# TensorE's program as loops of two heads, with paired buffers, quartered bias windows and 64-wide near products

## The reference

```python
attn = jnp.einsum('bhid,bhjd->bhij', q, k)
qL = jnp.einsum('bhid,hdm->bhim', q, rpe_k_table)
attn = attn + jnp.take_along_axis(qL, idx, axis=-1)
kL = jnp.einsum('bhjd,hdm->bhjm', k * scale, rpe_q_table)
attn = attn + jnp.swapaxes(jnp.take_along_axis(kL, idx, axis=-1), 2, 3)
attn = jax.nn.softmax(attn, axis=-1)
out = jnp.einsum('bhij,bhjd->bhid', attn, v)
S = jax.vmap(lambda a, seg: jax.ops.segment_sum(a, seg, num_segments=NUM_BUCKETS))(a_t, rp)
out = out + jnp.einsum('inbh,hnd->bhid', S, rpe_v_table)
```

## Time and profile before

| | us |
|---|---|
| runs | 1524.4, 1528.8 (median), 1531.9 |
| span of the profiled execution | 1522.0 |
| attention heads 0 to 29 | about 180 to 776 |
| experts | about 780 to 845 |
| heads 30 to 63 and projection | about 845 to 1522 |

### The profile page before, as it was taken

The page is one execution under the profiler, slowest core; times in us unless marked ns, Lnnn a source line. Parts: engine busy times, 40 slices in busy tenths (PEclk is TensorE's granted clock), DMA queues, the critical chain, the costliest instruction groups (busy, mean ns, idle before and its releaser), DMA issues. The chain is left out here.

```text
span 1522.0 us, 75140 instructions
## 1 busy us (share of the span) xinstructions
PE 1325.6 (87%) x32698; PEld 895.9 (59%) x32698; DVE 1111.2 (73%) x2461; ACT 797.9 (52%) x1408; POOL 541.3 (36%) x552
## 2 busy tenths in 40 slices
PE   2785399999999999988989899999999999999887
PEld 1352256666666666655668565666666666666555
DVE  7684378888888888887764676777777767777762
ACT  1332135655665666655541455665666555656544
POOL 3453212222222222222434244444444444444423
PEclk9897559999999999999995799999999999999999
DMA  4444546666556555554564566666666666666532
GB/s 97 138 142 138 159 158 200 200 207 193 186 183 191 190 176 183 181 184 153 174 189 145 160 183 182 183 192 198 186 183 196 183 176 180 190 183 183 149 104 58
DMA packets 167209, 260.10 MB, mean 171 GB/s; under 512 B 33980, under 2 KB 89397, under 8 KB 166886
## 3 DMA queue, kind: packets, MB, share of 16 engines
q1 hardware_dynamic: 155414, 248.46, 52.5%
q0 software_dynamic: 11472, 6.83, 3.7%
HBM read 145.14 MB, written 112.37 MB: 169 GB/s over the span
## 5 line engine op out<-in xcount | busy, mean ns | idle before, releaser
L1408 DVE TRANSPOSE_TENSOR_REDUCE tops<-PS 128x16 f32<-128x512 f32 x1024 | 689.7, 699 | 190.1 <-PE PS L697 183.9
L1096 ACT ACTIVATE PT<-PS 128x512 f32<-128x512 f32 x1024 | 590.2, 596 | 423.4 <-PE PS L697 416.1
L697 PE MATMUL PS<-Qs,Ks 73*32 73x512 bf16 (+29 forms) x11904 | 666.4, 322 | 66.8 <-DVE tops L1408 45.6
L697 PEld LDWEIGHTS PS<-Qs,Ks 73*32 73x32 bf16 (+1 forms) x11904 | 308.9, 97 | 266.7 <-DVE tops L1408 94.0
L697 PE MATMUL PS<-PT,Vst 128*9 128x256 f32 (+7 forms) x7552 | 345.4, 286 | 12.6 <-issue 12.1
L638 POOL COPY WP<-PT 128x768 f32<-128x768 f32 x128 | 105.3, 822 | 645.4 <-ACT PT L1096 460.9
L697 PE MATMUL PS<-WT,eye 96*32 96x96 bf16 (+2 forms) x4352 | 294.7, 206 | 0.2 <-issue 0.2
L697 PEld LDWEIGHTS PS<-PT,Vst 128*9 128x9 f32 x7552 | 187.8, 91 | 82.6 <-issue 32.3
L697 PEld LDWEIGHTS PS<-WT,eye 96*32 96x32 bf16 x4352 | 186.8, 99 | 22.5 <-issue 1.2
L657 POOL TENSOR_TENSOR ajp<-dq_s,ajp 128x508 bf16<-128x508 f32 x128 | 147.3, 1151 | 10.4
L626 POOL DMA_INDIRECT acc_d<-XNA,tok_i x64 | 100.8, 1575 | 78.8 <-DMA acc_d<-XNA,tok_i 66.2
(11 more groups left out here) (199 smaller groups left out, 1025.9 us busy)
## 6 DMA issues: line engine op xcount, KB each, us to landing
aj_d<-ajp SPq DMA_DIRECT2D x64, 768.0 KB
WT<-aj_d SPq DMA_DIRECT2D x192, 256.0 KB
dq_d<-dq_e SPq DMA_DIRECT2D x64, 512.0 KB, 5.3
dq_s<-dq_d SPq DMA_DIRECT2D x64, 512.0 KB, 3.9
TOE<-toe_d SPq DMA_DIRECT2D x33, 768.0 KB, 5.8
q_stack<-PT SPq DMA_DIRECT2D x24, 256.0 KB, 2.5
Qs<-q_stack SPq DMA_DIRECT2D x64, 96.0 KB
Ks<-k_stack SPq DMA_DIRECT2D x64, 96.0 KB
```

The lines of the kernel that those rows point to most:

```text
L697: return pe.matmul(o, l, r, start=start, stop=stop, skip_group_check=True)
L1096: act.activation(PT[:, TILE + N * J + 512 * half:TILE + N * J + 512 * half + 512], PS[:, 2 + u % 2, :], ACT.Exp).then_inc(s2_read, 1)
L1408: dve.tensor_reduce(tops[:, (h + 1) % 2, s // 2, 16 * (s % 2):16 * (s % 2) + 16], PS[:, s % 2, :].rearrange("p (c i) -> p c i", i=TILE), A ...
```

## The change

TensorE's program of heads 2 to 25 and 30 to 59 becomes two loops of 12 and 15 trips, two heads each (`pairs`); the other heads stay written out. Inside a loop all waits are against constants, so at the end of each trip 19 semaphores are counted down by a trip's worth, and the waits that follow the loop are lowered by what went (`own`). The few semaphores that others wait for too are compared with registers (heads_done, dq_turn, aj_turn, key_turn). All pauses are gone. A loop body must name fixed buffers, so these come in pairs: Q1, K1 for the first scores and Q2, K2 for the second, each loaded by five DMAs (`load_rows`); Qd, tabq (`load_dq`) and Ka, tabk (`load_aj`) single, for the bias operands, with two DMAs each; WT has two heads instead of three and is loaded in quarters of four slots, three DMAs each (`load_windows`), with rows of 512 bytes instead of 2048. aj_d has three copies instead of two. POOL's window copy waits for the values product instead of the exponentials. `near` has 24 products of 64 by 64 instead of 48 of 32 by 32, and Ym has 512 columns instead of 256.

```diff
-BLOCK = 1024
-PER_HEAD = 1007
-EXTRA = 9
-START = 58
-RAMP = 54
 LAG = 6
-RING = 5
+PAIR = 2
+CHUNKS = 4
...
-        Qs = sb("Qs", [ROWS, RING, N], BF16)
-        Ks = sb("Ks", [ROWS, RING, N], BF16)
-        tab = sb("tab", [ROWS, RING, 2, P], BF16)
-        WT = sb("WT", [P, 3, 2 * N])
+        Q1 = sb("Q1", [ROWS, PAIR, N], BF16)
+        K1 = sb("K1", [ROWS, PAIR, N], BF16)
+        Q2 = sb("Q2", [ROWS, PAIR, N], BF16)
+        K2 = sb("K2", [ROWS, PAIR, N], BF16)
+        Qd = sb("Qd", [ROWS, N], BF16)
+        Ka = sb("Ka", [ROWS, N], BF16)
+        tabq = sb("tabq", [ROWS, P], BF16)
+        tabk = sb("tabk", [ROWS, P], BF16)
+        WT = sb("WT", [P, PAIR, 2 * N])
...
+            def load_rows(h, Qx, Kx, rows_in):
+                (b, hh), r = place(h), h % PAIR
                 tok = slice(b * N, b * N + N)
-                sp.dma_start(Qs[0:48, r, :], q_stack[hh * HD:hh * HD + HD, :, tok].rearrange("d n t -> (d n) t")).then_inc(stack_in[r], 16)
-                sp.dma_start(tab[0:48, r, :, :],
-                             tab_stack[hh * HD:hh * HD + HD, :, :, :].rearrange("d n v p -> (d n) v p")).then_inc(stack_in[r], 16)
-                sp.dma_start(Qs[ROW_M:ROW_M + 3, r, :], zero_d).then_inc(stack_in[r], 16)
-                sp.dma_start(Qs[ROW_M + 6:ROW_M + 12, r, :], q_far[hh, :, tok]).then_inc(stack_in[r], 16)
-
-            def load_keys(h):
-                (b, hh), r = place(h), h % RING
+                sp.dma_start(Qx[0:48, r, :], q_stack[hh * HD:hh * HD + HD, :, tok].rearrange("d n t -> (d n) t")).then_inc(rows_in, 16)
+                sp.dma_start(Kx[0:48, r, :], k_stack[hh * HD:hh * HD + HD, :, tok].rearrange("d n t -> (d n) t")).then_inc(rows_in, 16)
+                sp.dma_start(Qx[ROW_M + 6:ROW_M + 12, r, :], q_far[hh, :, tok]).then_inc(rows_in, 16)
+                for m, row in ((0, ROW_M + 3), (1, ROW_M + 12)):
+                    sp.dma_start(Kx[row:row + 3, r, :], k_far[hh, 3 * m:3 * m + 3, tok]).then_inc(rows_in, 16)
...
+            def load_dq(h):
+                b, hh = place(h)
                 tok = slice(b * N, b * N + N)
-                sp.dma_start(Ks[0:48, r, :], k_stack[hh * HD:hh * HD + HD, :, tok].rearrange("d n t -> (d n) t")).then_inc(keys_in[r], 16)
-                for m, row in ((0, ROW_M + 3), (1, ROW_M + 12)):
-                    sp.dma_start(Ks[row:row + 3, r, :], k_far[hh, 3 * m:3 * m + 3, tok]).then_inc(keys_in[r], 16)
+                sp.dma_start(Qd[0:48, :], q_stack[hh * HD:hh * HD + HD, :, tok].rearrange("d n t -> (d n) t")).then_inc(qd_in, 16)
+                sp.dma_start(tabq[0:48, :], tab_stack[hh * HD:hh * HD + HD, :, 0, :].rearrange("d n p -> (d n) p")).then_inc(qd_in, 16)
+
...
+            def load_windows(t, q):
+
+                if not 0 <= t < HEADS:
+                    return
+                sp.wait_ge(aj_out, 16 * (t + 1))
+                wait(sp, s2_ready, SLOTS * (t - 2) + 4 * q + 4)
+                if t == 1:
+                    sp.wait_ge(s1_ready, 4 * q + 1)
+                for part in range(3):
+                    sp.dma_start(WTb[TILE * part:TILE * part + TILE, t % PAIR, :, 2 * q:2 * q + 2, :].rearrange("p s j n -> p s (j n)"),
+                                 shear(t % 3, part, 2 * q, 2)).then_inc(wt_in[q], 16)
...
+                if on(4):
+                    wait(sp, dq_psum, h + 4)
+                    load_dq(h + 4)
+                load_windows(h + 1, 2)
                 if on(0):
 
                     sp.wait_ge(mparts_ready, h + 1)
                     for n in range(3):
-                        sp.dma_start(Qs[ROW_M + n:ROW_M + n + 1, h % RING, :].rearrange("p (c j) -> p c j", j=TILE),
+                        sp.dma_start(Q2[ROW_M + n:ROW_M + n + 1, h % PAIR, :].rearrange("p (c j) -> p c j", j=TILE),
                                      mparts[:, n, :]).then_inc(mrow_in, 16)
+                if on(2):
+                    if h + 1 >= 0:
+                        sp.wait_ge(s1_ready, SLOTS * (h + 1) + 1)
+                    load_rows(h + 2, Q1, K1, rows1_in)
+                load_windows(h + 1, 3)
                 if on(4):
-                    wait(sp, s2_ready, SLOTS * h)
-                    load_queries(h + 4)
-                if on(2):
-                    t = h + 2
-                    sp.wait_ge(aj_out, 16 * (t + 1))
-                    wait(sp, s2_ready, SLOTS * h)
-                    for part in range(3):
-                        sp.dma_start(WTb[TILE * part:TILE * part + TILE, t % 3, :, :, :].rearrange("p s j n -> p s (j n)"),
-                                     shear(t % 2, part)).then_inc(wt_in[t % 3], 16)
-                if on(4):
-                    load_keys(h + 4)
+                    wait(sp, aj_psum, 2 * (h + 4))
+                    load_aj(h + 4)
+                if on(1):
+                    if h >= 0:
+                        sp.wait_ge(s2_ready, SLOTS * h + 1)
+                    load_rows(h + 1, Q2, K2, rows2_in)
...
+                load_windows(h + 2, 0)
                 if on(3):
                     t = h + 3
                     sp.wait_ge(aj_parts, 2 * t + 2)
-                    if t > 1:
-                        sp.wait_ge(wt_in[(t - 2) % 3], 48 * ((t - 2) // 3 + 1))
-                    sp.dma_start(aj_d[t % 2].rearrange("n p x -> p n x"), ajp[:, :, :, :].rearrange("p n j d -> p n (j d)")).then_inc(aj_out, 16)
+                    if t > 2:
+                        sp.wait_ge(s1_ready, SLOTS * (t - 3) + 13)
+                    sp.dma_start(aj_d[t % 3].rearrange("n p x -> p n x"), ajp[:, :, :, :].rearrange("p n j d -> p n (j d)")).then_inc(aj_out, 16)
...
                     sp.wait_ge(dq_copied, h + 5)
-                    wait(sp, dq_in, 16 * (h + 4))
+                    wait(sp, aj_psum, 2 * (h + 4))
                     sp.dma_start(dq_d[:, 64:64 + N], dq_e[:, :]).then_inc(dq_out, 16)
+                load_windows(h + 2, 1)
...
-                pool.wait_ge(s2_read, SLOTS * h + 8 * part + 8)
+                pool.wait_ge(pv_done, NJ * h + 4 * part + 4)
...
-            def near(h):
-
-                for b, k in [(8 + 8 * q + a, 0) for a in range(8) for q in range(4)] + [(b, -1) for b in range(8)] + [(b, 1) for b in range(40, 48)]:
-                    to = (b - 8) % 32
-                    q, a = to // 8, to % 8
+            def near():
+
+                edges = [x for b in range(4) for x in ((b, -1), (20 + b, 1))]
+                for b, k in [(4 + 8 * g + a, 0) for a in range(8) for g in range(2)] + edges:
+                    g, a = divmod((b - 4) % 16, 8)
                     J0, J1 = max(0, -k), min(NJ, NJ - k)
-                    ins = mm(PS[TILE * q:TILE * q + TILE, 6, 32 * a + 4 * (J0 + k):32 * a + 4 * (J1 + k)],
-                             TOE[:, SPAN - 4 * b - 4:SPAN - 4 * b, :].rearrange("p a b -> p (a b)"), WP[:, J0:J1, 4 * b:4 * b + 4],
+                    ins = mm(PS[64 * g:64 * g + 64, 6, 64 * a + 8 * (J0 + k):64 * a + 8 * (J1 + k)],
+                             TOE[:, SPAN - 8 * b - 8:SPAN - 8 * b, :].rearrange("p a b -> p (a b)"), WP[:, J0:J1, 8 * b:8 * b + 8],
                              start=k == 0 and a == 0)
...
+                    if s == 13 and looped and h < hm:
...
-                    if s == 11 and h in (-4, -3, -2):
-                        pause(RAMP)
-                    if s >= 12 and h >= 0:
-                        spare = BLOCK - PER_HEAD - (EXTRA if j_r == 2 else EXTRA + 1 if h == LISTS else 0)
-                        pause(spare // 4 + (s - 12 < spare % 4))
...
+            def pairs(h, n, keys_done):
+
+                pe.reg_mov(heads_done, h)
...
+                with nc.Fori(0, n, engines=[pe.engine], hint_back_edge=True, head_slot={pe.engine: 0}):
+                    iteration(h, True)
+                    iteration(h + 1, True)
+                    pe.sem_inc(s1_read, -2 * SLOTS)
+                    pe.sem_inc(s2_read, -2 * SLOTS)
+                    pe.sem_inc(rows1_in, -2 * ROWS_IN)
+                    pe.sem_inc(rows2_in, -2 * ROWS_IN)
+                    for q in range(CHUNKS):
+                        pe.sem_inc(wt_in[q], -2 * WINDOWS)
+                    pe.sem_inc(mrow_in, -2 * 48)
+                    pe.sem_inc(v_ready, -2)
+                    pe.sem_inc(o_copied, -2)
+                    pe.sem_inc(top_ready, -2)
+                    pe.sem_inc(top_read, -2)
+                    pe.sem_inc(on_ready, -2)
+                    pe.sem_inc(ym_ready, -2)
+                    pe.sem_inc(dq_in, -2 * 16)
+                    pe.sem_inc(toe_in, -16)
+                    pe.sem_inc(qd_in, -2 * TABLES)
+                    pe.sem_inc(ka_in, -2 * TABLES)
+                gone[0] += 2 * n
+
+            for h in range(-4, 2):
+                iteration(h, False)
+            pairs(2, (LISTS - 1) // 2, 1)
+            for h in range(LISTS + 1, hm):
+                iteration(h, False)
...
+            pairs(hm, (HEADS - 4 - hm) // 2, 4)
+            for h in range(HEADS - 4, HEADS + 2):
```

(7 more changed lines are left out.)

266 lines of the change are left out of this document (153 added, 113 removed).

## The result

The changed kernel takes 1723.5 us (median of 4 runs, 1718.6 to 1726.6) against 1530.3 for the kernel before on the same chip: 1.127 times as long, 95% interval 1.123 to 1.131. The forecast was 1559, and its range ended at 1615. The sign was right, the size was not: +30 us were forecast, +193 came. Times are medians of all runs of a kernel, while every ratio leaves out runs more than 1.5% above that kernel's fastest, so the two can differ a little.

A forecast was written before the change was run, and what follows sets the result against it. Bound: TensorE and VectorE in the first stretch, the dq round trip by DMA in the second. +20 (loop end) -7 -3 +21 (SP) -1 = +30 us on 1522.0: 1552, or 1559 in runs; range 1515 to 1615.

The forecast's parts named there:

- Part 3: TensorE, end of each pair of heads: 19 decrements and a branch cost +1.7 us per pair, +20 us in 12 pairs.
- the 0.7 us hidden under the wait for the head maximum: TensorE at the loop's end: 0.67 us per head of waiting for VectorE's maximum was taken to hide decrements.
- Part 1: TensorE's pauses taken out: mostly under queued work, a gain of 0.2 us per head.
- The 1 us taken for the start: Pauses ahead of head 0: removing them gains 1 us for the whole start, bounds 0 and 8.1.
- Part 2: Near products on TensorE: 48 passes two side by side take 1.3 us, a gain of 0.1 to 0.2 us per head.
- rival 5: Near products: 64-wide ones run one after another, 2.6 in place of 1.45 us; about 1610 us, chance 0.07.
- The 4 us named beside that rule: Near products: if a tiling-mode drain cost as much as their gain, the sum would be 4 us higher.
- Part 4: SP's queue: 32 DMAs per head instead of 16 make it late, +0.7 us for 30 heads, +21 us.
- The pace of 19.41 us: Heads 2 to 29, from VectorE's one reduction per head: 19.41 us per head before the change.
- rivals 4 and 6: TensorE code: late at back edges, 1605 up to 1650, chance 0.10; fetches stay some 264, 3 us move, no chance given.
- Rivals 1 and 2: TensorE decrements hidden, SP keeps up: about 1504 us, chance 0.15; half of each, no change: 1529, chance 0.13.
- Rival 3: SP's queue saturated: four stalls per head, +50 us over now, 1585 to 1595 us, chance 0.15.

The follow-up runs named there:

- e2: The changed kernel with its 19 decrements per trip spread over the second head of the loop body: 1602.6 us, ratio 1.045 to the kernel before.
- e3: The kernel before, without loops, with 19 of each two heads' pauses put in a row behind the odd head's slot 15: 1659.5 us, ratio 1.081.
- e5: The kernel before with all its pauses taken out and nothing else changed: 1621.9 us (1593.4 to 1631.6) against 1522.5.
- e12: The kernel before with 14 pauses per head in place of 17, so 1021 instructions a head instead of 1024: 1724.0 us, ratio 1.119.
- e1: The changed kernel with both loops written out again, without decrements, branch or registers: 1728.9 us, ratio 1.129 to the kernel before.
- e11: The changed kernel with decrements spread, Qd, tabq and third window quarter loaded behind the maxima rows, row loads on ScalarE in slots 6 to 10: 1576.3 us, ratio 1.032.
- e6: The kernel before with each head's three bias window loads issued as twelve, in quarters, at the same place of SP's queue: 1670.9 us, ratio 1.099.
- e7: The changed kernel with decrements spread, and on SP the Qd, tabq and third window quarter loads moved behind the maxima rows: 1651.9 us, ratio 1.087.
- e8: The kernel before, without loops, with 14 of each two heads' pauses put in a row behind the odd head's slot 15: 1580.3 us, ratio 1.035.
- e4: The kernel before, without loops, with 10 of each two heads' pauses put in a row behind the odd head's slot 15: 1556.2 us, ratio 1.017.

## Why the prediction was wrong, point by point

**Part 3, closing a loop: the step that failed.** Its account of the stretch is right: 19 decrements at 0.15 us, an idle stretch of 2.5 us (2 to 3 was forecast), once per two heads. Its price was +1.7 us per pair. A pair took 45.5 us in place of 38.5 in the first stretch, 7 more; taking the row apart (e2) gave back 4.4 and 4.9 us a pair in the two stretches. Idle time rose by 2.9 us a pair, with the longer waits for dq_s in it. What the step put at nothing is the clock: TensorE then runs mostly for some 10 us at half clock. The kernel before, whose idle stretches in this part are all under 2 us, had shown a fall only behind three of them, for 3.4 us each. e2 shows the size (92 of the 126 us that it gives back are busy time), and e3 shows the fall without any loop. One term of the step's own sum was misread too: the 0.7 us hidden under the wait for the head maximum are waits of the weight loads; TensorE itself waited for that maximum only 4.4 us in the 24 heads of the first stretch.

**Part 1, the pauses.** The step priced them as time that goes away, -0.2 us a head. What it left out is their count, which by e5 and e12 sets where the pieces of code end in every head: +71 us in the fastest run without any of them (e5), +189 us with three fewer per head (e12). In the changed kernel the loops' code is not fetched again, so the error hardly showed in its time. e1 has straight code without pauses, and may be slow in part by this; its trace does not show it. The 1 us taken for the start came out as 2 by the reduction of head 0 (196.0 us for 198.4), but e5 without any pause had 198.6, so this is not shown to be the pauses.

**Part 2, the near products.** The 48 passes last 1.61 us from the first start to the last end, against 1.63 in the earlier trace rows:

```profile
483.12 1.61 PE L721 MATMUL PS<-WP,TOE 128*64 128x64 f32 x48
```

In medians of the first stretch it is 1.61 against 1.68, a gain of 0.07 us where 0.1 to 0.2 was forecast, and rival 5 (one after another, 2.6 us) is out. The rule of the Trainium skill (TensorEngine Tiling (Array Packing), Key Properties) that changing the tiling mode drains TensorE can be neither seen nor ruled out here: no run has the same passes without a change of width. The 4 us named beside that rule do not fit the 0.1 us of the sum, which make 2.4 in 24 heads. The masking on VectorE went from 0.425 to 0.69 us, less than the doubling allowed for the earlier trace rows, and lies under other work.

**Part 4, SP's queue.** The size came out near by luck, the mechanism is not the one named. +21 us were forecast for the second stretch; rearranging the transfers in e11 gave 20 there, and 17 in the first, where none was forecast. But in the changed kernel SP is not full, and dq_d goes out 0.2 us (median) after its copy; it even lands sooner than before, in 4.8 us where the earlier trace rows have 5.7. It is dq_s that lands late, above all in heads with TOE (6.5 us for 4.6). Part 4 let the last window group and TOE "fit in" the wait for dq_d. As time on SP they do; but the transfers they start are then under way beside dq_s, and the step took the landings as changed by 0.5 us at most. Its own mechanism, the queue late at dq_d, is real and dear in e6 and e7.

**The sum.** +20 and +21 for parts 3 and 4 became 110 to 125 us for the row and 20 to 35 for the transfers (7.2 to 8.2 and 1.3 to 2.3 points of 1530). The rest lies in heads 26 to 29 and the experts (+20 us by the VectorE reductions), among it the entry of the second loop, and in what e11 has left in the stretches (+19 us). The pace of 19.41 us that the prediction gives for heads 2 to 29 is that of heads 1 to 28, which changes nothing in the sum.

**The rivals.** Fetches fell from 264 packets to 58, so rivals 4 and 6 are out; the entry of a loop waits 6.3 us once, a back edge not at all (e2). The Trainium skill (Runtime: NRT & Kernel Launch, Instruction fetch mechanics) gives TensorE's instruction memory as 2048 instructions; the packet count agrees with a body of about 1850 staying in it. Rivals 1 and 2 asked for the decrements to be hidden; even hidden (e2, e11) the kernel stays above the one before. Rival 3 (SP saturated) did not happen; its two paces make +67 us and not the +50 written there, which is the top of its range of 1585 to 1595. None had the clock in it.

## What to carry over

Look at the granted clock behind every idle stretch of TensorE, and price a new stretch of about 2 us with what the matmuls after it lose, which here was more than the stretch itself; bookkeeping that closes a loop belongs spread through the body, one instruction at a time. A filler that seems to do nothing may hold the program's length per round, so change its count by a few before taking it out. With a DMA round trip in the pace, ask of every added transfer not only when its queue gets to it but what it flies beside, and look at the landings head by head, since a median over two groups hides both.

## What the runs showed of the hardware

- An idle stretch of TensorE at full clock was followed by half clock in 25 of 27 cases at 2.4 to 2.7 us (changed kernel), 26 of 30 at 2.1 to 2.4 us (e3), 13 of 26 at 1.5 to 1.8 us (e8), and in none of 31 at 0.9 to 1.2 us (e4). The half clock lasted 3.4 us at the least, 10.2 us in 16 of the 25 cases of the changed kernel.
- A straight program of 1021 instructions a head in place of 1024 had a late piece of code of 2.2 to 3.1 us in each of 25 heads in a row (e12), at the same 264 packets.
- A taken branch back to the start of a body of two heads costs TensorE at most 0.6 us (e2). The first entry of the second loop, behind the experts, cost 6.1 to 6.4 us (changed kernel, e2, e11), that of the first loop 2.3 to 4.4.
- A transfer of 512 KB (dq_s) lands in 3.5 us when no large transfer is under way and nothing is issued right behind it (e7, e11, heads without TOE), in 4.0 to 4.7 with five transfers or more issued right behind (changed kernel, e2), and in 5.3 to 5.9 us with a 768 KB transfer issued some 1 us ahead (e11, heads with TOE). In e2, with both, it takes 6.1 to 6.6. No run moved the 768 KB transfer alone.
- Nineteen semaphore decrements in a row on TensorE take 2.8 us and leave it idle for 2.5. Spread over a head (e2) they leave no such stretch: all idle time put down to "issue" in the second loop's 30 heads is 9.3 us, 6.1 of it the loop's entry.
